# Values and transposed probabilities of four attention layers in high and low fp32r parts, three weights' low parts made by GpSimd

## The reference, cut to what matters

```python
def _sparse_attention(x, src, dst, wq, bq, wk, bk, wv, bv, wo, bo):
    N, D = x.shape
    H, Dh = (NUM_HEADS, D // NUM_HEADS)          # 4 heads of 128
    q = (x @ wq + bq).reshape(N, H, Dh) * Dh ** (-0.5)
    k = (x @ wk + bk).reshape(N, H, Dh)
    v = (x @ wv + bv).reshape(N, H, Dh)
    scores = jnp.einsum('ehd,ehd->eh', q[src], k[dst])
    smax = jax.ops.segment_max(scores, src, num_segments=N)
    ex = jnp.exp(scores - smax[src])
    denom = jax.ops.segment_sum(ex, src, num_segments=N)
    attn = ex / denom[src]
    out = jax.ops.segment_sum(attn[:, :, None] * v[dst], src, num_segments=N)
    return out.reshape(N, D) @ wo + bo

for i in range(NUM_BLOCKS):                      # 4 layers
    y = _cond_layer_norm(x, cond, s1_w[i], s1_b[i], b1_w[i], b1_b[i])
    y = _sparse_attention(y, src, dst, wq[i], bq[i], wk[i], bk[i], wv[i], bv[i], wo[i], bo[i])
    x = x + y
    y = _cond_layer_norm(x, cond, s2_w[i], s2_b[i], b2_w[i], b2_b[i])
    y = jax.nn.relu(y @ m_w1[i] + m_b1[i]) @ m_w2[i] + m_b2[i]
    x = x + y
```

## Time and profile before

| | us |
|---|---|
| median of 3 runs | 1388.12 (1388.08 to 1390.32) |
| the profiled execution, its device time | 1389.13 |
| its span, first to last instruction | 1387.2 |
| PE busy | 1169.0 (84%) |
| DVE busy | 860.2 (62%) |
| ACT busy | 455.9 (33%) |
| POOL busy | 267.1 (19%) |

### The profile page before, as it was taken

How to read it: one execution, slowest core, us unless ns; L and a number is a source line. 1 busy time by engine, 2 the same in 40 slices (tenths; PEclk the granted TensorE clock), 3 DMA queues, 4 the chain that set the end, 5 groups by cost and what they waited for, 6 DMA issues and landing times.

```text
span 1387.2 us, 15086 instructions
## 1 busy us (share of the span) xinstructions
PE 1169.0 (84%) x5730; PEld 892.4 (64%) x5730; DVE 860.2 (62%) x1522; ACT 455.9 (33%) x673; POOL 267.1 (19%) x313
## 2 busy tenths in 40 slices
PE   5987733668879997899889998899899998879983
PEld 2645521334458975897769877798678877646552
DVE  6586732566554258566666656667656567946885
ACT  1101630000014442445224343246224442315771
POOL 1157448888400001000110000100100001110001
PEclk9998856789989998899999999999999999778897
DMA  5236886212031142020010201011000220100001
GB/s 177 67 96 188 272 274 140 49 34 50 4 122 46 40 128 103 4 99 25 31 61 1 99 25 61 31 61 62 30 31 31 99 61 31 38 0 1 1 1 37
DMA packets 47903, 93.96 MB, mean 68 GB/s; under 512 B 17200, under 2 KB 17600, under 8 KB 46418
## 3 DMA queue, kind: packets, MB, share of 16 engines
q1 hardware_dynamic: 27338, 71.77, 16.2%
q0 software_dynamic: 20480, 20.99, 6.5%
HBM read 74.65 MB, written 17.91 MB: 67 GB/s over the span
## 4 chain that ended last, share of the span: by engine, by line
PE 63%; DVE 14%; POOL 9%; issue 5%; ACT 5%; DMA 3%; SPq 0%; DVEq 0%; POOLq 0%; ACTq 0%
PE ps L1473 15%; PE ps L1526 14%; PE ps L1501 9%; POOL logit_ring L581 6%; PE ps L1506 5%; PE ps L1660 4%; PE ps L1560 4%; POOL arena L575 3%; PE ps L1606 2%; DMA logits_scratch<-arena 2%; PE ps L1631 2%; PE ps L1489 2%; DVE arena L1182 1%; ACT arena L775 1%; DVE weight_low L1152 1%
## 5 line engine op out<-in xcount | busy, mean ns | idle before, releaser
L1473 PE MATMUL ps<-arena 125*128 125x314 f32 (+5 forms) x820 | 228.1, 463 | 14.6 <-DVE neg_max L1021 10.6
L1473 PEld LDWEIGHTS ps<-arena 125*128 125x128 f32 (+5 forms) x820 | 145.0, 191 | 87.2 <-DVE neg_max L1021 15.0
L559 POOL TENSOR_TENSOR var_eps<-mean_var,ln_consts 125x1 f32<-125x1 f32 x70 | 15.9, 227 | 949.1 <-DVE mean_var L1168 582.7
L1631 PE MATMUL ps<-arena 125*125 125x512 f32 x192 | 123.3, 736 | 75.3 <-DVE arena L1050 61.4
L575 POOL DMA_INDIRECT arena<-value_scratch,src_idx x80 | 100.6, 1258 | 76.0 <-issue 33.4
L581 POOL DMA_INDIRECT logit_ring<-logits_scratch,pair_idx x80 | 106.7, 1334 | 24.4 <-issue 24.4
L1560 PE MATMUL ps<-ident,arena 125*125 125x125 f32 x625 | 81.0, 284 | 15.6 <-ACT arena L851 7.7
L1560 PEld LDWEIGHTS ps<-ident,arena 125*125 125x125 f32 x625 | 75.9, 195 | 25.1 <-ACT arena L851 9.0
L1631 PEld LDWEIGHTS ps<-arena 125*125 125x125 f32 x192 | 33.7, 220 | 77.7 <-issue 77.5
L1632 PEld LDWEIGHTS ps<-arena 125*125 125x125 f32 x192 | 41.1, 214 | 57.1 <-issue 57.1
L1501 PE MATMUL ps<-input_high,weight_high 128*128 128x314 f32 x320 | 73.1, 310 | 2.4 <-DVE weight_low L1152 2.4
(11 more groups left out here) (267 smaller groups left out, 2612.5 us busy)
## 6 DMA issues: line engine op xcount, KB each, us to landing
logits_scratch<-arena SPq DMA_DIRECT2D x5, 2187.5 KB
arena<-in_m_w SPq DMA_DIRECT2D x8, 1024.0 KB, 6.5
arena<-in_w_up SPq DMA_DIRECT2D x4, 1024.0 KB, 5.7
arena<-in_w_down SPq DMA_DIRECT2D x4, 1024.0 KB, 7.5
arena<-in_wq SPq DMA_DIRECT2D x4, 1024.0 KB, 5.2
arena<-in_wk SPq DMA_DIRECT2D x4, 1024.0 KB, 5.2
arena<-in_wv SPq DMA_DIRECT2D x4, 1024.0 KB, 5.2
arena<-in_wo SPq DMA_DIRECT2D x4, 1024.0 KB, 5.3
```

The lines of the kernel that those rows point to most:

```text
L1473: last = mm(out_view[:, place:place + HALF_W], w, r[:, lo:lo + HALF_W], start=n == 0, stop=n == len(pairs) - 1 and not open_end)
L1631: mm(ps[0:TILE, 512 * j:512 * j + 512], onehot, VG[slot][:, u, :], start=False, stop=True, skip_group_check=True)
```

## The change

- **Values.** The value rows now go to V32, which lies where "attended_low" was. ACT writes their high parts (VH, three instructions, `values_high`), DVE their low parts (VL, three instructions, `values_low`).
- **Transposed probabilities.** ACT writes the high part of all five tiles of a head (PTH, `transposed_high`), DVE the low part of all five (PTL, `transposed_low`), which also releases the slot. PTH and PTL hold one head each in place of the two heads of PT.
- **The product.** `weigh(h)` is 30 fp32r matmuls of 314 columns in place of ten in fp32. The first 20 need PTH alone, the last ten PTL.
- **Three weights.** The low parts of wo, m1 and m2 are made by POOL behind the powers of the first norm of the layer, and leave DVE's list.
- **Places.** The low part of the attention's output moves to the region of the queries. The rest is padding.

```diff
-        PT = at(R_PT, 2, NT, W, p=TILE)
+        PT = at(R_PT, 2, NT * W + 4, p=TILE)[:, :, 0:NT * W].rearrange("p b (j n) -> p b j n", j=NT)
...
-        OL, OH = over("attended_low", R_O, [128, FT, W], f32r), over("attended_high", R_Y, [128, FT, W], f32r)
+        OL, OH = over("attended_low", R_Q, [128, FT, W], f32r), over("attended_high", R_Y, [128, FT, W], f32r)
+        OL0 = over("attended0_low", R_O, [128, FT, W], f32r)
+        V32 = at(R_O, NT, D, p=TILE)
+        VH, VL = over("value_high", R_V, [128, NT, D], f32r), over("value_low", R_O, [128, NT, D], f32r)
+        PTH, PTL = (over(name, R_PT + (NT * W + 4) * n, [128, NT, W], f32r) for n, name in enumerate(("probs_high", "probs_low")))
...
-            for n in range(2 * LAYERS):
-                powers((sig("var_ready1"), sig("rstd_ready1")), pool_chain, n * NT)
+            def weight_low(name, layer):
+                pool.wait_ge(sig(name + "_high"), layer + 1)
+                n = SLOT[name]
+                g.tensor_tensor(WLOW[n][:, :, :], WEIGHT[n], WHIGH[n][:, :, :].bitcast(f32), ALU.subtract
+                                ).then_inc(sig(name + "_low"), 1)
+
+            for i in range(LAYERS):
+                powers((sig("var_ready1"), sig("rstd_ready1")), pool_chain, 2 * i * NT)
+                for name in ("wo", "m1", "m2"):
+                    weight_low(name, i)
+                powers((sig("var_ready1"), sig("rstd_ready1")), pool_chain, (2 * i + 1) * NT)
...
-                def transposed(h):
-                    for j in (0, 2, 4):
+                def transposed_high(h):
+                    for j in range(NT):
                         B.wait_filled(act, ("pt", i, h, j))
-                        B.release(("pt", i, h, j), a.activation(tiled(PT[:, h % 2, j, :]), B.blocks(("pt", i, h, j), NT), ACT.Copy))
+                        a.activation(tiled(PTH[0:TILE, j, :]), B.blocks(("pt", i, h, j), NT), ACT.Copy).then_inc(sig("probs_high"), 1)
+
+                def values_high():
+                    for n, pair in enumerate(PAIRS):
+                        B.wait_evacuated(act, ("v", i, n))
+                        tiles = slice(pair[0], pair[-1] + 1)
+                        a.activation(VH[0:TILE, tiles, :], V32[:, tiles, :], ACT.Copy).then_inc(sig("values_high"), 1)
...
                 query_key_high(3)
-                transposed(0)
+                values_high()
+                transposed_high(0)
                 exps(2)
...
-                def transposed(h):
-                    for j in (1, 3):
-                        B.wait_filled(dve, ("pt", i, h, j))
-                        B.release(("pt", i, h, j), v.tensor_copy(tiled(PT[:, h % 2, j, :]), B.blocks(("pt", i, h, j), NT)))
+                def transposed_low(h):
+                    for j in range(NT):
+                        dve.wait_ge(sig("probs_high"), NT * (H1 * i + h) + j + 1)
+                        B.release(("pt", i, h, j), v.tensor_tensor(tiled(PTL[0:TILE, j, :]), B.blocks(("pt", i, h, j), NT),
+                                                                   tiled(PTH[0:TILE, j, :]).bitcast(f32), ALU.subtract))
+
+                def values_low(n):
+                    dve.wait_ge(sig("values_high"), 3 * i + n + 1)
+                    tiles = slice(PAIRS[n][0], PAIRS[n][-1] + 1)
+                    v.tensor_tensor(VL[0:TILE, tiles, :], V32[:, tiles, :], VH[0:TILE, tiles, :].bitcast(f32), ALU.subtract
+                                    ).then_inc(sig("values_low"), 1)
...
-                    row_bias(B, ("v", i, n), pair, V, ROWS[:, 0:1, :])
+                    row_bias(B, ("v", i, n), pair, V32, ROWS[:, 0:1, :])
                     if n == 0:
                         normalise(1)
-                transposed(0)
+                    else:
+                        values_low(n - 1)
+                values_low(2)
+                transposed_low(0)
                 masked(2)
-                weight_low("wo", i)
                 attended_low(0)
-                transposed(1)
+                transposed_low(1)
                 normalise(2)
                 masked(3)
-                weight_low("m1", i)
                 attended_low(1)
-                transposed(2)
+                transposed_low(2)
                 normalise(3)
-                weight_low("m2", i)
                 attended_low(2)
-                transposed(3)
+                transposed_low(3)
                 attended_low(3)
...
                     key = ("av", i, h)
                     B.claim(pe, key)
-                    B.fill(wide(B.view(key, 128), [(V[:, j, 128 * h:128 * (h + 1)], PT[:, h % 2, j, :]) for j in range(NT)],
-                                out_of_psum(B, "pt", i, h)))
+                    part, out_view = slice(128 * h, 128 * (h + 1)), B.view(key, 128)
+                    for j in range(NT):
+                        pe.wait_ge(sig("probs_high"), NT * (H1 * i + h) + j + 1)
+                        for values in (VH, VL):
+                            for place, lo in ((0, 0), (512, HALF_W)):
+                                mm(out_view[:, place:place + HALF_W], values[0:TILE, j, part], PTH[0:TILE, j, lo:lo + HALF_W],
+                                   start=j == 0 and values is VH, stop=False)
+                    for j in range(NT):
+                        B.wait_evacuated(pe, ("pt", i, h, j))
+                        for place, lo in ((0, 0), (512, HALF_W)):
+                            last = mm(out_view[:, place:place + HALF_W], VH[0:TILE, j, part], PTL[0:TILE, j, lo:lo + HALF_W],
+                                      start=False, stop=j == NT - 1)
+                    B.fill(last)
```

More of the change, by code:

```diff
@@ L161, in build @@
         R_PT = R_P + 2 * NT * W
-        R_LC = R_PT + 2 * NT * W
+        R_LC = R_PT + 2 * NT * W + 8
         R_C = R_LC + NT * W
@@ L798, in _ @@
                 outputs(0)
-                transposed(1)
+                transposed_high(1)
                 exps(3)
@@ L802, in _ @@
                 outputs(1)
-                transposed(2)
+                transposed_high(2)
                 weight_high("m2", i)
                 outputs(2)
-                transposed(3)
+                transposed_high(3)
                 outputs(3)
@@ L1075, in _ @@
                 dve.wait_ge(sig("evacuated_high"), k + 1)
-                A.release(("at", k), v.tensor_tensor(tiled(OL[:, k, :]), A.blocks(("at", k), NT, 128),
+                A.release(("at", k), v.tensor_tensor(tiled(OL0[:, k, :]), A.blocks(("at", k), NT, 128),
                                                      tiled(OH[:, k, :]).bitcast(f32), ALU.subtract))
@@ L1157, in _ @@
             dve.wait_ge(sig("x1_ready"), NT)
-            v.memset(PT[:, :, :, NODES:W], 0.0).then_inc(sig("padding_ready"), 1)
+            v.memset(PTL[0:TILE, :, NODES:W].bitcast(f32), 0.0).then_inc(sig("padding_ready"), 1)
             dve.wait_ge(sig("padding_ready"), 1)
@@ L1317, in _ @@
                         B.wait_filled(dve, ("v", i, n))
-                        pads(dve, v.memset(PT[:, 0, :, NODES:W], 0.0))
-                    row_bias(B, ("v", i, n), pair, V, ROWS[:, 0:1, :])
+                        pads(dve, v.memset(PTH[0:TILE, :, NODES:W].bitcast(f32), 0.0))
+                    row_bias(B, ("v", i, n), pair, V32, ROWS[:, 0:1, :])
                     if n == 0:
                         normalise(1)
-                transposed(0)
+                    else:
+                        values_low(n - 1)
+                values_low(2)
+                transposed_low(0)
                 masked(2)
-                weight_low("wo", i)
                 attended_low(0)
-                transposed(1)
+                transposed_low(1)
                 normalise(2)
                 masked(3)
-                weight_low("m1", i)
                 attended_low(1)
-                transposed(2)
+                transposed_low(2)
                 normalise(3)
-                weight_low("m2", i)
                 attended_low(2)
-                transposed(3)
+                transposed_low(3)
                 attended_low(3)
@@ L1430, in _ @@
                 row_bias(B, ("wx", n), pair, V, ROWS[:, 0:1, :])
-            pads(dve, v.memset(PT[:, 0, :, NODES:W], 0.0))
+            pads(dve, v.memset(PT[:, :, :, NODES:W], 0.0))
             for h in range(H3):
@@ L1639, in _ @@
             pe.wait_ge(sig("biases_ready"), 1)
-            split_rows(A, ("o",), OH, OL, WHIGH[2], WLOW[2], out_of_psum(A, "at"), bias=0)
+            split_rows(A, ("o",), OH, OL0, WHIGH[2], WLOW[2], out_of_psum(A, "at"), bias=0)
             pe.wait_ge(sig("counts_back"), 32)
@@ L1802, in _ @@
                 make_scores(2)
-                for n in range(3):
-                    B.wait_evacuated(pe, ("v", i, n))
+                pe.wait_ge(sig("values_low"), 3 * (i + 1))
                 weigh(0)
```

## The result

The changed kernel takes 1412.96 us (median of four runs, 1410.27 to 1414.86) against 1388.78 of the kernel before in the same job (one set of runs on one chip): 1.0167 times as long, 95% interval 1.0147 to 1.0188. The forecast was 1404.5 with a range of 1385.5 to 1409. The direction and the mechanism came, but not the size: 24 us slower, where 16 were forecast, and above the range.

The account below looks back on a forecast made before the run. PE was taken to bound the attention's second half, with a DVE and ACT chain nearly as long. 4 x 4.1 = 16.4 us on the profiled 1389.1 gave 1405.5, against the median 1404.5; range 1385.5 to 1409.

Parts of the forecast that it names:

- PE's saving per head: Head product on PE: 30 fp32r matmuls take 4.36 us where the fp32 product took 5.30, 0.94 us less a head.
- the walk: Layer 1's attention followed engine by engine from 777.29: gain 0.4 to -0.1 us a layer without collision, 0.2 taken.
- the collision: POOL's m2 subtraction meets DVE's five tensor_scalar of head 3 ahead of turn 3 and holds them up: +4.3 us.
- The tensor_scalar of head 2: Sign: if these are held up too, POOL's subtraction is longer than 5 us and the time is above the range.
- the term for the clock: Behind PE's pause of 4.5 us the granted clock may fall to the lower level, adding up to 1 us a layer.
- Nothing collides: POOL and DVE run side by side, or DVE's five tensor_scalar hold POOL off: 1387.3 us, chance 0.27.
- PE's saving arrives: The low parts are no bound and the slots do not wait: 1373 us, a part of it 1384; chance 0.15.
- The point given for it: The mask of head 3 starting before 797.5 in layer 1's time decides for the faster case.

Follow-up runs that it names:

- e1: The changed kernel, but POOL makes m2's low part only after the last tensor_scalar of head 3: 1385.0 us, 0.9988 of the kernel before.
- e8: e6 with the values' low parts made by POOL and ACT's high part of the last value tile behind transposed_high(0): 1369.9 us, 0.9879 of the kernel before.
- e3: The changed kernel with m2's low part made by four POOL instructions of 512 columns in place of one of 2048: 1411.7 us, 1.0178 of the kernel before.
- e5: The kernel before, fp32 product kept, with the low parts of wo, m1 and m2 made by POOL: 1397.4 us, 1.0074 of the kernel before.
- e2: The changed kernel with 28 extra fp32r matmuls, results overwritten, between product 2 and turn 3: 1401.0 us, 1.0111 of the kernel before.
- e6: The changed kernel with heads 2 and 3 normalised earlier on DVE, POOL's wo waiting for head 2's normalisation, m1 and m2 for head 3's: 1376.6 us, 0.9911.

## Why the prediction was right and wrong

**Right: PE's saving per head.** 30 matmuls take 2.92 + 1.45 = 4.37 us in the changed kernel, 4.36 forecast.

**Right: the walk.** The second mask starts at 801.59 - 3.30 = 798.3 (798.0 forecast), the tensor_scalar of head 3 at 810.30 (810.3). The walk gave a gain between 0.4 and -0.1 us a layer without a collision; e1's undisturbed layers are 0.1 longer than before. I had taken 0.2 of gain, where the lower end was right. PE waits at tile 4 of turn 0 (1.2 us, about 1 forecast) and at the last score tile of head 3 (1.8, about 2). These waits are where the larger part of the saving went, not all of it: in e1's layer 1 PE waits 3.4 us in the stretch, 1.2 before, which is 2.2 of the 3.8. The rest is in turns, scores and the last two products, which take longer than the rows of before say (e8); the walk did not have it as such.

**Right: the collision, its place and nearly its size.** 6.67 us for the five tensor_scalar, 6.6 forecast (810.3 to 816.9). POOL's subtraction takes 4.66 there, where I took 4.2 from a copy; it starts 0.2 us earlier against DVE than I let it, and the tensor_scalar end 0.2 sooner behind it, which evens this out. The Trainium skill's rule (SBUF — State Buffer, "Who interferes with whom"), that the second of such a pair blocks for the whole instruction, agrees with the one tensor_scalar of 4822 ns, with e3's turns of 1.54 us and with e5's small product. The Trainium skill's 4497 ns for a tensor_tensor add of 2048 elements (GPSIMD Engine Reference, "Performance versus the Vector engine") is 1 to 4% under the 4556 to 4657 ns of the changed kernel's subtractions. The tensor_scalar of head 2 were not held up (0.54 to 0.55), and the time is above the range all the same, which the prediction had tied to them.

**Wrong: the term for the clock.** The prediction put it as "up to 1 us a layer", in the upper part of the range and not in the forecast. From the end of the tensor_scalar to the rows of wo it is 9.61 us in the changed kernel's layer 1 (820.27 to 829.88) and 7.82 in e1 (811.04 to 818.86), 1.8 us more, with a granted clock of 0.51 where e2, its PE busy, shows turn 3 at the usual pace. In the four layers it is 2.4, 1.8, 2.2 and 1.7 us more. In layer 2 the clock had fallen at the second mask as well, which I had not thought of for a pause of 1.8 us: turn 3 starts 1.3 us later than in layer 1. Together 9.3 us, 2.3 a layer. With the collision's 4 x 4.3 = 17.2 and the walk's 0.5, this is 27.0, which is what the four stretches of the changed kernel are longer than those before. The span grew by 22.5 only. The 4.5 between lie outside the stretches and were not explained: 3.1 of them ahead of the last row bias of layer 0. That point comes at 615.4 us in the trace of before and between 610.8 and 614.9 in the nine others, whatever the kernel, so it says little of the change; it hid a part of the miss.

So the failed step is the clock's term of the sum: it stood at nothing in the forecast and at 1 us a layer at most in the range, and it measured 2.3. The pause was priced by its length alone. I had seen that the pause would be 4.5 us and that the clock could fall, and bounded the price with a guess in place of a row. The row was there. At the start of layer 2 of before, behind waits of 0.5 to 1.0 us for the norm, matmuls of 314 columns start 0.26 us apart, and 2 us later 0.14 to 0.15:

```profile
846.21 0.47 PE L1736 MATMUL ps<-input_high,weight_low 128*128 128x314 f32 x1
846.47 0.46 PE L1735 MATMUL ps<-input_high,weight_high 128*128 128x314 f32 x1
...
848.60 0.30 PE L1736 MATMUL ps<-input_high,weight_low 128*128 128x314 f32 x1
848.74 0.30 PE L1735 MATMUL ps<-input_high,weight_high 128*128 128x314 f32 x1
```

Turn 3 is 2.99 us at the upper level; at half the clock it is up to twice that, so 2 to 3 us a layer would have been the term, and the sum 1412.5 to 1416.5 (an estimate made afterwards).

**Rivals.** "Nothing collides" did not happen in the changed kernel; its time is e1's, to 0.3 us a layer in the walk's terms. "PE's saving arrives" needs e6's and e8's order, and 2.2 us of 3.8 arrive there. The point given for it, the mask of head 3 before 797.5 in the old layer's time, was not reached by the change (798.3) and is reached by e6 (795.5).

## What to carry to other kernels

Before work is given to GpSimd because it has time, look at what VectorE does in the microseconds in which the new instruction will run: a tensor_scalar from SBUF to SBUF, or a product with both operands in SBUF, waits until the GpSimd instruction is over, and a subtraction with one operand in PSUM does not (e1). If the two meet, a wait on the GpSimd side costs nothing when its result is needed late (e1: 25 us by the ratios, for one wait). A pause of TensorE costs its length and then the clock of what runs next, so price both; and a saving on the busiest engine only counts once the order of the others has been made to match (e6, e8); e8 still gets only 2.2 of 3.8 us a layer.

## What the runs showed of the hardware that was not expected

- Splitting the GpSimd instruction does not give VectorE room. The engines take turns, each tensor_scalar waits for one piece (1.54 us in place of 0.54), and four pieces take 5.81 us beside it, one whole 4.66.
- A pause of TensorE of 1.8 us behind a dense stretch is followed by a lower clock in some layers and not in others of one execution (e1: 44.24 us in layers 0 and 3, 42.97 in 1 and 2). A pause of 2.5 us was followed by it in three layers of four (e5), one of 4.3 to 4.5 us in all eight of the changed kernel and e3.
- Throw-away matmuls in a forced pause can pay: 28 of them a layer gave back 8 us (e2, with 2 to 13 left open by the two intervals).
